# Last down-projection in Else branches, and the final normalisation in two steps, in a fused recurrent-attention and mixture-of-experts kernel

## The chip, the cores and the metric

One core of one Trainium2 chip runs the kernel. The metric is device time in microseconds, the median over runs of the same program. Engines: TensorE (PE; its weight loads are shown as PEld), VectorE (DVE), ScalarE (ACT), GpSimd (POOL) and SyncE (SP).

## What is computed

A block of 2 x 1024 tokens of width 256 is normalised by row. The normalised rows go two ways, and both results are added to the input.

```python
x = L0_attn_hidden_states
xn = _layernorm(x, axis=-1)
x = x + _L0_attn_ref(xn, ...) + _L0_ffn_ref(xn, ...)
# attention part, a recurrence along time in logarithms:
log_h = a_star + jax.lax.cumlogsumexp(log_values - a_star, axis=1)
log_h = (log_h - log_h.mean()) / jnp.std(log_h, ddof=1)
x = jnp.exp(log_h)[:, 1:, :] + hidden_states
return (x - mu) * jax.lax.rsqrt(var + LN_EPS) * ln_w + ln_b
# mixture of experts, top 2 of 8, FFN width 704:
h = jax.nn.silu(x @ w1[e].T) * (x @ w3[e].T)
out = out + h @ w2[e].T * expert_weight
```

## The kernel before

The rows of the 2048 tokens, each picked by two experts, are sorted by expert into tiles of 128 rows. How many tiles there are depends on the data: at least SURE = 33, at most NTILES = 39; here 36 are used, tiles 0 to 35. DVE works this number out on the chip and writes it to `tiles`.

For each tile j, POOL gathers its rows from `xn_dram` into `work` (`gather`, line 390, four tiles ahead); PE transposes them (`x_tile`); ACT and DVE split them into a high and a low part (`x_hi`, `x_lo`, line 967); PE does the up-projection (`up`, line 1301); ACT applies SiLU (line 608) and DVE multiplies (`gate`, line 976); PE transposes the product (`h_tile`, line 1331); ACT and DVE split it again (`h_hi`, line 603, and `h_lo`, line 971); PE does the down-projection one tile later (`down(j - 1)` in tile j, line 1319); ACT copies it with the row weights (`y_copy`, line 634), and POOL scatters it to the result with an adding indirect DMA (`scatter`, line 406). Each scatter waits for the landing of the one before, through the semaphore `s_st`.

Each engine has its own instruction queue, written out by hand in program order. Tiles 1 to 32 are unrolled. In between, the attention part runs on the same queues: `between(j)` and `after(j)` put its steps before or behind h_lo(j) on DVE. Its last step, `last_norm(m)` for m = 0 to 7, normalises two groups of 128 rows each with four operations (two of line 1069, two of line 1074) and counts up `s_p2`. When a quarter of the result is finished, POOL adds it to `out` with a plain adding DMA (`add_attention`, line 414), which waits for the last scatter, and the next scatter waits for the addition. Before the change this is done at tiles 28 (two quarters), 30 and 32 (one each). Where POOL works on an addition, the low parts of the next expert's weights (`split_due`, line 425, one piece at a time) go ahead of the scatter.

Tiles 33 to 38 are nested tests (`tail`, line 300): each engine compares the number of used tiles with j and does tile j if it is larger. The last tile's down-projection, copy and scatter come behind the whole nest, with the number of used tiles in a register: `last_down` (12 filling matmuls of line 1181, then `down`), `last_copy` (lines 736 and 739) and `end` (lines 464 to 472, the scatter at line 470).

## Time and profile before

| what | us |
|---|---|
| median of 3 runs | 352.63 (350.98 to 352.78) |
| the profiled execution's own time | 352.66 |
| its span in the profile | 350.8 |
| PE busy | 323.4 (92%) |
| DVE busy | 243.4 (69%) |
| ACT busy | 229.2 (65%) |
| POOL busy | 204.4 (58%) |

The span runs from the first to the last instruction of the program; the execution's time has some 1.8 us more around it. Busy shares are averages over stages, and what a stage waits for is read from the timeline and the chain of waits.

### The profile page before, as it was taken

The page shows a single profiled execution, that of the slowest core. Times are in us where ns is not written, and L with a number is a line of the kernel's source. Part 1 is how long each engine was busy: PE and PEld are TensorE (multiplying, and loading weights), DVE is VectorE, ACT ScalarE, POOL GpSimd, SP SyncE. Part 2 cuts the span into 40 slices and gives each one's busy share as a digit, 9 for nine tenths or more (in the row PEclk, how much of TensorE's full clock was granted, in tenths as well). Part 3 has the DMA queues.
Part 4 walks back from the last instruction along what each step waited for, and adds up shares of the span by engine and source line. Part 5 has one row for each costly group of instructions (what it writes and reads, how often), then busy time and mean ns, then how long its engine had stood idle before and what let it go on. Part 6 is the DMA issues. An engine that isn't in the chain of part 4 may idle for free.

```text
span 350.8 us, 6683 instructions
## 1 busy us (share of the span) xinstructions
PE 323.4 (92%) x1964; PEld 272.7 (78%) x1964; DVE 243.4 (69%) x430; ACT 229.2 (65%) x365; POOL 204.4 (58%) x137
## 2 busy tenths in 40 slices
PE   8998999898999999899989899999999999999950
PEld 8773474587878889788878788789998997999940
DVE  5488778989996779959889942455498767553410
ACT  2548898564889993899974349963955565443420
POOL 4600004249977763897789927765398458863531
PEclk9999969999999999999999999999999999999995
DMA  7952922005434642345346432544265265456431
GB/s 258 347 215 94 308 87 60 17 0 160 101 98 92 167 97 48 76 101 141 58 87 164 98 56 41 142 105 101 33 157 139 61 77 92 50 90 84 56 49 15
DMA packets 19087, 37.01 MB, mean 105 GB/s; under 512 B 2272, under 2 KB 13536, under 8 KB 19008
## 3 DMA queue, kind: packets, MB, share of 16 engines
q0 software_dynamic: 9168, 11.97, 21.7%
q1 hardware_dynamic: 8496, 22.56, 20.7%
q10 hardware_dynamic: 1376, 1.85, 1.5%
q8 instruction: 29, 0.48, 0.6%
q14 instruction: 18, 0.15, 0.1%
HBM read 27.45 MB, written 11.03 MB: 110 GB/s over the span
## 4 chain that ended last, share of the span: by engine, by line
PE 28%; issue 17%; ACT 15%; DVE 15%; DMA 13%; POOL 6%; POOLq 2%; ACTq 2%; DVEq 0%
PE PS L1301 9%; DMA out<-work,sidx 7%; PE PS L1195 7%; DMA out<-xrow 5%; PE PS L1319 4%; ACT L718 3%; POOL work L390 2%; PE PS L1331 2%; POOL out L406 2%; DVE tmp L976 2%; ACT tmp L608 2%; ACT L710 2%; ACT wbuf L617 2%; DVE hT L971 2%; DVE A L1013 1%
## 5 line engine op out<-in xcount | busy, mean ns | idle before, releaser
L1301 PE MATMUL PS<-wbuf,xT 128*128 128x512 f32 (+1 forms) x648 | 148.0, 382 | 4.4 <-issue 3.5
L1301 PEld LDWEIGHTS PS<-wbuf,xT 128*128 128x128 f32 x648 | 117.2, 188 | 28.3 <-issue 8.7
L425 POOL TENSOR_TENSOR wbuf<-raw,wbuf x28 | 78.7, 2822 | 27.4 <-ACT wbuf L617 26.6
L406 POOL DMA_INDIRECT out<-work,sidx x35 | 62.2, 1778 | 46.9 <-ACT work L634 24.8
L1319 PE MATMUL PS<-wbuf,hT 128*128 128x256 f32 x648 | 86.8, 288 | 0.0
L1319 PEld LDWEIGHTS PS<-wbuf,hT 128*128 128x128 f32 x648 | 79.3, 189 | 1.9 <-issue 1.9
L390 POOL DMA_INDIRECT work<-xn_dram,gidx x39 | 51.2, 1312 | 50.2 <-DVE gidx L907 36.8
L971 DVE TENSOR_TENSOR hT<-PS,hT 128x768 fp32r<-128x768 f32 x36 | 34.2, 950 | 46.1 <-ACT hT L603 45.1
L608 ACT ACTIVATE tmp<-PS 128x512 f32<-128x512 f32 x72 | 31.6, 459 | 38.8 <-PE PS L1301 38.7
L976 DVE TENSOR_TENSOR tmp<-tmp,PS 128x512 f32<-128x512 f32 x72 | 34.9, 515 | 28.8 <-ACT tmp L608 27.9
L1331 PE MATMUL PS<-ident,tmp 128*128 128x128 f32 x216 | 30.2, 276 | 6.1 <-DVE tmp L976 6.0
L634 ACT ACTIVATE work<-PS,wrow 128x256 f32<-128x256 f32 x35 | 16.4, 469 | 29.3 <-PE PS L1319 29.3
L603 ACT ACTIVATE hT<-PS 128x768 fp32r<-128x768 f32 x35 | 28.3, 810 | 10.5 <-PE PS L1331 10.5
L617 ACT ACTIVATE wbuf<-raw x28 | 30.4, 1110 | 4.7 <-issue 4.6
L1195 PE MATMUL PS<-xnT_M,small_sb 128*128 128x512 f32 x64 | 31.0, 624 | 1.7 <-ACT tmp L528 1.0
L1331 PEld LDWEIGHTS PS<-ident,tmp 128*128 128x128 f32 x216 | 23.9, 141 | 8.7 <-DVE tmp L976 7.7
L1195 PEld LDWEIGHTS PS<-xnT_M,small_sb 128*128 128x128 f32 x64 | 12.1, 202 | 14.0 <-issue 12.8
L710 ACT ACT_TABLE_LOAD x14 | 18.0, 1283 | 0.3
L718 ACT ACT_TABLE_LOAD x14 | 18.0, 1283 | 0.2
L967 DVE TENSOR_TENSOR xT<-PS,xT 128x256 fp32r<-128x256 f32 x37 | 15.5, 418 | 0.1
L575 ACT ACTIVATE xT<-PS 128x256 fp32r<-128x256 f32 x37 | 14.0, 382 | 1.6 <-PE PS L1270 1.6
L581 ACT ACTIVATE wrow<-work,first_pick 128x1 f32<-128x1 f32 x37 | 14.1, 385 | 0.0
(186 smaller groups left out, 367.3 us busy)
## 6 DMA issues: line engine op xcount, KB each, us to landing
raw<-w_main SPq DMA_DIRECT2D x24, 544.0 KB, 4.0
raw<-w_main SPq DMA_DIRECT2D x8, 416.0 KB, 3.5
xn_dram<-xrow SPq DMA_DIRECT2D x4, 516.0 KB, 5.9
out<-xrow POOLq DMA_DIRECT2D x4, 512.0 KB, 6.5
xrow<-x ACTq DMA_DIRECT2D x4, 256.0 KB, 5.8
xrow<-x SPq DMA_DIRECT2D x4, 256.0 KB, 5.2
small_sb<-small ACTq DMA_DIRECT2D x1, 768.0 KB, 8.3
work<-xn_dram,gidx POOLq DMA_INDIRECT x39, 4.1
```

The costliest lines, as they stand in the source:

```text
L390: pool.indirect_dma_start(xg[:, k, :], None, xn_dram, bass.IndirectOffsetOnAxis(gidx[:, j:j + 1], 0)).then_inc(s_gt[k], 16)
L406: pool.indirect_dma_start(out, bass.IndirectOffsetOnAxis(sidx[:, j:j + 1], 0), ysb[:, j % DEEP, :], None, compute_op=ALU.add).then_inc(s_s ...
L425: pool.tensor_tensor(lo, raw[:, ds(part, WP)], hi.bitcast(fp32), ALU.subtract).then_inc(s_w, 1)
L608: act.activation(sls[n], w1_ps[n], ACT.Silu).then_inc(s_silu, 1)
L617: act.activation(wslot(p // PIECES + 1, 0, part), raw[:, ds(part, WP)], ACT.Copy).then_inc(s_hi, 1)
L718: act.preload_act_table_set("silu_and_others")
L971: dve.tensor_tensor(hT[:, 1, :], hT_ps, hT[:, 0, :].bitcast(fp32), ALU.subtract).then_inc(s_hlo, 1)
L976: dve.tensor_tensor(g_hs[n], sls[n], w3_ps[n], ALU.mult).then_inc(s_g, 1)
L1195: ins = pe.matmul(PS[:, base + qo * CH:base + (qo + 1) * CH], wzh_sb[:, q, mat, qo * P:(qo + 1) * P], xnT[:, q, c * CH:(c + 1) * CH], star ...
L1301: ins = pe.matmul(PS[:, at:at + cols], xT[:, slot, xpart, q * P:(q + 1) * P], wbuf[:, w, wpart, q * 2 * F + at:q * 2 * F + at + cols], sta ...
L1319: ins = pe.matmul(y_ps, hT[:, hpart, c * P:(c + 1) * P], wbuf[:, w, wpart, W13 + c * D:W13 + (c + 1) * D], start=(c == 0 and hpart == 0 an ...
L1331: ins = pe.transpose(hT_ps[:, c * P:(c + 1) * P], g_h[:, a:a + P], ident[:, :])
```

## The change

Each end test gets an Else branch. If tile j isn't needed, the down-projection, copy and scatter of tile j - 1 stand in that branch with constant numbers; the same three stand behind tile 38 for the case that all tiles are used. The 12 filling matmuls, the copies of the row weights and of the scatter column, and the waits on register values go. On DVE, last_norm(6) moves from behind h_lo(30) to before it, and last_norm(7) from behind h_lo(31) to behind h_lo(30). On POOL, the third and the fourth quarter of the attention result are added together at tile 31, not at tiles 30 and 32.

```diff
-        def tail(eng, tile, end=None, drain=None):
+        def tail(eng, tile, end=None):
...
                     if j + 1 < NTILES:
                         nest(j + 1)
-                    if drain:
-                        drain(j)
+                    elif end:
+                        end(NTILES)
                     eng.nop(nofuse=True)
+                if end:
+                    with eng.Else():
+                        end(j)
+                        eng.nop(nofuse=True)
             nest(SURE)
-            if end:
-                end(used)
+            return used
...
-                    if j in (28, 30, 32):
-                        added = j // 2 - 12
+                    if j in (28, 31):
+                        added += 2
                         add_attention(j - 1, before, added)
                     done = tile(i, u, done, added, added > before)
...
             def end(used):
+
                 for k in range(DEEP):
-                    pool.wait_ge(s_gt[k], 16 * len(range(k, SURE + DEEP, DEEP)))
-                pool.tensor_copy(scol[:, 0:1], sidx[:, ds(used - 1, 1)]).then_inc(s_sc, 1)
...
-                hold(pool, s_st, whole * 16)
-                hold(pool, s_y, used + 1)
-                pool.indirect_dma_start(out, bass.IndirectOffsetOnAxis(scol[:, 0:1], 0),
-                                        hst[:, 0:D], None, compute_op=ALU.add).then_inc(s_st, 16)
-                hold(pool, s_st, 16 * used)
-            tail(pool, tile, end, drain)
+                    pool.wait_ge(s_gt[k], 16 * len(range(k, min(used + DEEP, NTILES), DEEP)))
+                scatter(used - 1, PARTS_OF_H)
+            used = tail(pool, tile, end)
+            hold(pool, s_st, 16 * used)
...
-            def last_copy(used):
-                hold(act, s_ws, used)
-                act.activation(wrow[:, NCOL:NCOL + 1], wrow[:, ds(used - 1, 1)], ACT.Copy).then_inc(s_wl, 1)
-                act.wait_ge(s_wl, 1)
-                hold(act, s_dn, used)
-                act.activation(hst[:, 0:D], y_ps, ACT.Copy, scale=wrow[:, NCOL:NCOL + 1]).then_inc(s_y, 1)
-            tail(act, tile, last_copy)
+            tail(act, tile, lambda used: y_copy(used - 1))
...
                 if 20 <= j <= 27:
                     row_stats(j - 20)
+                if j == 30:
+                    last_norm(6)
...
-                if 24 <= j <= 31:
+                if 24 <= j <= 29:
                     last_norm(j - 24)
+                if j == 30:
+                    last_norm(7)
...
-            def last_down(used):
-                warm(LAST_FILL)
-                down(used - 1, pe.snap(r_before, min_val=0, max_val=E - 1))
-            tail(pe, tile, last_down)
+            tail(pe, tile, lambda used: down(used - 1, pe.snap(r_before, min_val=0, max_val=E - 1)))
```

DVE's queue around tile 30, before: from gate(30) to h_lo(31). The names are those of the tiles in memory; hT<-PS,hT is h_lo, xT<-PS,xT is x_lo, and xrow holds the rows that last_norm works on.

```order
L976 TENSOR_TENSOR tmp<-tmp,PS 128x512 [waits silu_ready]
L976 TENSOR_TENSOR tmp<-tmp,PS 128x192 [waits silu_ready]
L967 TENSOR_TENSOR xT<-PS,xT 128x256 [waits x_hi_ready]
L971 TENSOR_TENSOR hT<-PS,hT 128x768 [waits h_hi_ready]
L1069 SCALAR_TENSOR_TENSOR xrow<-xrow,mv,small_sb 128x256 x2
L1074 SCALAR_TENSOR_TENSOR xrow<-xrow,rstd,small_sb 128x256 [waits last_norm_steps]
L1074 SCALAR_TENSOR_TENSOR xrow<-xrow,rstd,small_sb 128x256
L976 TENSOR_TENSOR tmp<-tmp,PS 128x512 [waits silu_ready]
L976 TENSOR_TENSOR tmp<-tmp,PS 128x192 [waits silu_ready]
L967 TENSOR_TENSOR xT<-PS,xT 128x256 [waits x_hi_ready]
L971 TENSOR_TENSOR hT<-PS,hT 128x768 [waits h_hi_ready]
```

The same place of DVE's queue now, from gate(30) to gate(31); lines are those of the changed kernel.

```order
L957 TENSOR_TENSOR tmp<-tmp,PS 128x512 [waits silu_ready]
L957 TENSOR_TENSOR tmp<-tmp,PS 128x192 [waits silu_ready]
L948 TENSOR_TENSOR xT<-PS,xT 128x256 [waits x_hi_ready]
L1050 SCALAR_TENSOR_TENSOR xrow<-xrow,mv,small_sb 128x256 x2
L1055 SCALAR_TENSOR_TENSOR xrow<-xrow,rstd,small_sb 128x256 [waits last_norm_steps]
L1055 SCALAR_TENSOR_TENSOR xrow<-xrow,rstd,small_sb 128x256
L952 TENSOR_TENSOR hT<-PS,hT 128x768 [waits h_hi_ready]
L1050 SCALAR_TENSOR_TENSOR xrow<-xrow,mv,small_sb 128x256 x2
L1055 SCALAR_TENSOR_TENSOR xrow<-xrow,rstd,small_sb 128x256 [waits last_norm_steps]
L1055 SCALAR_TENSOR_TENSOR xrow<-xrow,rstd,small_sb 128x256
L957 TENSOR_TENSOR tmp<-tmp,PS 128x512 [waits silu_ready]
L957 TENSOR_TENSOR tmp<-tmp,PS 128x192 [waits silu_ready]
```

Eight operations of the normalisation, four before h_lo(30) and four behind it, now stand between x_lo(31) and gate(31), and none behind h_lo(31).

POOL's queue behind the last end test, before: the end of the nest, then the last scatter (line 470).

```order
L300 UNCONDITIONAL_BRANCH x4
L300 UNCONDITIONAL_BRANCH [waits gathered2]
L300 UNCONDITIONAL_BRANCH [waits gathered1]
L464 ISA [waits gathered2,gathered3,gathered1,gathered0]
L464 COPY scol<-sidx 128x1
L467 TENSOR_LOAD tiles_whole [waits attention_added,scatter_column_ready]
L467 ISA x2
L292 REGISTER_ALU
L292 REGISTER_ALU [waits rows_added]
L470 DMA out<-hst,scol 2176x256 [waits y_copied]
```

POOL's queue now, two of the seven places where the last scatter stands (those of the last two Else branches), and the final wait.

```order
L404 DMA out<-work,sidx 2176x256 [waits rows_added,gathered3,attention_added,gathered2,y_copied,gathered1,gathered0]
L303 UNCONDITIONAL_BRANCH
L295 UNCONDITIONAL_BRANCH
L404 DMA out<-work,sidx 2176x256 [waits rows_added,gathered3,attention_added,gathered2,y_copied,gathered1,gathered0]
L303 UNCONDITIONAL_BRANCH
L287 REGISTER_ALU
L58 UNCONDITIONAL_BRANCH [waits rows_added]
```

The copy of the column, the load of a number of tiles and the register steps between the waits are gone; one DMA with constant waits is left in each branch. On PE each Else branch holds both variants of a down-projection, 18 matmuls each, so six more blocks of 36 matmuls now stand behind the tile bodies.

## Rows read from the trace of the kernel before

**Rows 1.** The page's slices: TensorE busy and its clock, tenths in 40 slices

```profile
PE   8998999898999999899989899999999999999950
PEclk9999969999999999999999999999999999999995
```

**Rows 2.** Timeline of the end: start us, us, engine, line, operation, tiles, [idle before]

```profile
327.42 0.47 ACT L634 ACTIVATE work<-PS,wrow 128x256 f32<-128x256 f32 x1 [1.48 <-PE PS L1319]
...
334.07 0.82 PE L1331 MATMUL PS<-ident,tmp 128*128 128x128 f32 x6
334.27 0.47 ACT L634 ACTIVATE work<-PS,wrow 128x256 f32<-128x256 f32 x1 [1.48 <-PE PS L1319]
...
335.77 0.96 DVE L971 TENSOR_TENSOR hT<-PS,hT 128x768 fp32r<-128x768 f32 x1 [2.79 <-ACT hT L603]
...
337.50 0.84 PE L1181 MATMUL PS<-ones_b 128*128 128x128 bf16 x12 [2.62 <-issue]
337.84 1.56 POOL L406 DMA_INDIRECT out<-work,sidx  x1 [2.51 <-DMA out<-work,sidx]
...
338.19 2.38 PE L1319 MATMUL PS<-wbuf,hT 128*128 128x256 f32 x18
...
340.66 0.47 ACT L739 ACTIVATE hst<-PS,wrow 128x256 f32<-128x256 f32 x1 [3.69 <-PE PS L1319]
342.63 1.57 POOL L470 DMA_INDIRECT out<-hst,scol  x1 [3.02 <-DMA out<-work,sidx]
```

**Rows 3.** Chain of waits at the end: start us, us, what

```profile
337.84 3.90 DMA out<-work,sidx
...
341.91 0.50 issue
342.41 0.04 POOLq L292
342.44 0.19 issue
```

**Rows 4.** Timeline of POOL, tiles 28 to 33

```profile
283.79 2.73 POOL L414 DMA_DIRECT2D out<-xrow  x2 [2.77 <-DMA out<-work,sidx]
...
294.54 1.66 POOL L406 DMA_INDIRECT out<-work,sidx  x1 [0.51 <-issue]
...
310.32 1.80 POOL L406 DMA_INDIRECT out<-work,sidx  x1 [1.73 <-issue]
...
318.96 1.38 POOL L414 DMA_DIRECT2D out<-xrow  x1 [2.86 <-DMA out<-work,sidx]
...
325.58 1.64 POOL L406 DMA_INDIRECT out<-work,sidx  x1 [3.87 <-issue]
...
329.66 1.58 POOL L406 DMA_INDIRECT out<-work,sidx  x1 [1.12 <-DMA out<-work,sidx]
```

**Rows 5.** Line 300 (end tests) and line 1284 behind it, PE's sequencer: ns min/median/max

```profile
L300 PEldq COMPARE_BRANCH  x4: 65/68/4413, 313.0 to 333.0; - x4
...
L1284 PEldq COMPARE_BRANCH  x2: 75/134/194, 338.1 to 338.4; - x2
```

**Rows 6.** Chain of waits at tile 29: scatter(28)

```profile
298.64 3.76 DMA out<-work,sidx
```

**Rows 7.** Timeline of DVE and POOL, tiles 28 to 30

```profile
288.52 3.16 DVE L1074 SCALAR_TENSOR_TENSOR xrow<-xrow,rstd,small_sb 128x256 f32<-128x256 f32 x2
288.82 5.22 POOL L425 TENSOR_TENSOR wbuf<-raw,wbuf  x2 [0.92 <-ACT wbuf L617]
...
294.96 0.87 DVE L1069 SCALAR_TENSOR_TENSOR xrow<-xrow,mv,small_sb 128x256 f32<-128x256 f32 x2
295.87 0.88 DVE L1074 SCALAR_TENSOR_TENSOR xrow<-xrow,rstd,small_sb 128x256 f32<-128x256 f32 x2
...
298.27 0.42 DVE L967 TENSOR_TENSOR xT<-PS,xT 128x256 fp32r<-128x256 f32 x1
...
299.81 3.00 POOL L425 TENSOR_TENSOR wbuf<-raw,wbuf  x1
...
301.48 0.96 DVE L971 TENSOR_TENSOR hT<-PS,hT 128x768 fp32r<-128x768 f32 x1 [2.79 <-ACT hT L603]
```

**Rows 8.** Chain of waits at tile 27: copy to scatter, landing to addition

```profile
278.15 0.48 ACT work L634
...
278.67 0.53 issue
...
283.21 0.58 issue
```

**Rows 9.** Busy time by stretch, PE; before the DMA share stands the granted clock

```profile
334.90:337.50 2.60, 0.00 (x0) 0.00 (x0) 0.96 (x1) 1.01 (x2) 0.43 (x1) 1.00 0.49 65
...
340.60:342.60 2.00, 0.00 (x0) 0.00 (x0) 0.00 (x0) 0.47 (x1) 0.00 (x0) 1.00 0.26 39
342.70:350.80 8.10, 0.00 (x0) 0.00 (x0) 0.00 (x0) 0.00 (x0) 1.51 (x1) 0.50 0.14 16
49.40:52.50 3.10, 3.09 (x4) 1.50 (x5) 0.50 0.00 0
57.00:60.00 3.00, 2.95 (x7) 1.33 (x7) 1.00 0.34 88
```

More of the change, by code:

```diff
@@ L48 @@
 FILL = 8
-LAST_FILL = 12
 BIG = 3.0e38
@@ L123, in build_program @@
         first_pick = sb("first_pick", [P, NCOL])
-        wrow = sb("wrow", [P, NCOL + 1])
+        wrow = sb("wrow", [P, NCOL])
         slot_i = sb("slot_i", [P, 3, 2 * NT], i32)
-        scol = sb("scol", [P, 1], u32)
         gidx = sb("gidx", [P, NCOL], u32)
@@ L130, in build_program @@
         tiles = sb("tiles", [P, 1], i32)
-        tiles_whole = sb("tiles_whole", [P, 1], i32)
         plan = sb("plan", [P, NCOL + 1], i32)
@@ L216, in build_program @@
         s_ws = sem("row_weights_ready")
-        s_wl = sem("last_row_weights_ready")
         s_fill = sem("x_copied_to_result")
@@ L248, in build_program @@
         s_gt = [sem(f"gathered{k}") for k in range(DEEP)]
-        s_sc = sem("scatter_column_ready")
         s_xt = sem("x_tile_transposed")
@@ L451, in _ @@
                     before = added
-                    if j in (28, 30, 32):
-                        added = j // 2 - 12
+                    if j in (28, 31):
+                        added += 2
                         add_attention(j - 1, before, added)
                     done = tile(i, u, done, added, added > before)
-            def drain(j):
-                if j + DEEP < NTILES:
-                    pool.wait_ge(s_gt[j % DEEP], 16 * ((j + DEEP) // DEEP + 1))
             def end(used):
                 for k in range(DEEP):
-                    pool.wait_ge(s_gt[k], 16 * len(range(k, SURE + DEEP, DEEP)))
-                pool.tensor_copy(scol[:, 0:1], sidx[:, ds(used - 1, 1)]).then_inc(s_sc, 1)
-                pool.wait_ge(s_sc, 1)
-                pool.wait_ge(s_ab, 16 * PARTS_OF_H)
-                whole = pool.value_load(tiles_whole[0:1, 0:1], min_val=SURE - 1, max_val=NTILES - 1)
-                hold(pool, s_st, whole * 16)
-                hold(pool, s_y, used + 1)
-                pool.indirect_dma_start(out, bass.IndirectOffsetOnAxis(scol[:, 0:1], 0),
-                                        hst[:, 0:D], None, compute_op=ALU.add).then_inc(s_st, 16)
-                hold(pool, s_st, 16 * used)
-            tail(pool, tile, end, drain)
+                    pool.wait_ge(s_gt[k], 16 * len(range(k, min(used + DEEP, NTILES), DEEP)))
+                scatter(used - 1, PARTS_OF_H)
+            used = tail(pool, tile, end)
+            hold(pool, s_st, 16 * used)
         @block.scalar
@@ L867, in tile_experts @@
                 step(dve.tensor_scalar(tiles[:, :], tend[:, E - 1:E], float(SURE), None, ALU.max))
-                step(dve.tensor_scalar(tiles_whole[:, :], tiles[:, :], -1, None, ALU.add))
                 dve.sem_inc(s_eid, 1)
```

## The prediction

> **What bounds the kernel now.** The page's slices come first [rows 1]: TensorE's clock stands at full nearly throughout, and only the last two slices are thin. So the body of the run belongs to TensorE, and what this change touches is the last 25 us and the two ends that meet there. The timeline of the end comes next [rows 2]. Call a tile's down-projection down(j); 36 tiles are used, 0 to 35. TensorE transposes tile 35 at 334.07 to 334.89, then does nothing until the 12 filling matmuls at 337.50, runs down(35) at 338.19 to 340.57, ScalarE copies it at 340.66 to 341.13, and GpSimd starts its scatter at 342.63. The copy was therefore ready 1.50 us before that scatter. The chain of waits says why [rows 3]: scatter(34) starts at 337.84, takes 3.90 to land, at 341.74, and only then do GpSimd's register waits and their 0.50 and 0.19 us of issue run. At the very end two queues race: scatters, one at a time, on GpSimd; and TensorE's end test with down(35) behind it. The scatters win by little. After 342.63 come 8.2 us (the landing, about 3.8, and the shutdown) that the change leaves alone.
>
> Where the scatters fell behind is seen on GpSimd's timeline [rows 4]. The last addition of the attention result is issued at 318.96 and scatter(31) follows at 325.58, 6.62 later. From there on one scatter follows the other at 329.66 - 325.58 = 4.08 us, less than the 6.85 us between the copies of two tiles (327.42 and 334.27 [rows 2]), so the backlog shrinks but is not gone by tile 35.
>
> TensorE's end test is one branch of 4413 ns begun at 333.0 [rows 5], so it ends at 337.45, where tests that fall through take 65 to 68 ns. It starts while the transposes are still queued; 2.6 us of it show as TensorE idle.
>
> **The change, part by part.** *Two additions instead of three.* Nothing moves before tile 30: the first pair is still issued at tile 28. GpSimd's schedule from there, worked out: scatter(28) starts at 298.64 and lands 3.76 later, at 302.40 [rows 6]; the weight piece it overlaps ends at 299.81 + 3.00 = 302.81 [rows 7]. At tile 30 no addition is due, so the gather (about 0.3 of gap, 1.0 of work, 0.3 of gap, as between the gathers and scatters of this engine) is followed by scatter(29) at about 304.5 instead of 310.32. It lands at 308.3, and the addition follows 0.6 later (283.17 to 283.79 in [rows 8]), at 308.9. Both parts go out together. The pair of tile 28 was issued at 283.79 and its scatter followed at 294.54 [rows 4], 10.75 later; I take that for this pair too. Its bounds are 6.62, if the second addition hides behind the first, and 2 x 6.62 = 13.2, if they share nothing. Scatter(30) is then at 308.9 + 10.75 = 319.7, and scatter(34), four steps on, at 319.7 + 4 x 4.08 = 336.0 instead of 337.84, landing at 339.9. With the bounds it lands between 339.4 (scatter(34) can't start before its copy, ready at 334.74, and 0.8 of issue) and 342.3.
>
> *Normalisation before h_lo(30).* VectorE idles 2.79 us ahead of h_lo(30), from 298.69 on [rows 7]. The four operations of last_norm(6) take 0.87 + 0.88 [rows 7] and would fit. But the last of them would start at about 299.9 (298.6 + 0.87 and half of 0.88), and GpSimd's weight piece starts at 299.81. What happens then stands in the same trace: at tile 28 the same pair of operations took 3.16 us instead of 0.88, with the piece starting at 288.82 in the middle of it [rows 7]. I take the blocked case: the operation ends with the piece, near 303.1, h_lo(30) starts 1.5 late, last_norm(7) runs to 305.7, and gate(31) starts at 305.6, over a microsecond late. Behind that gate wait the transposes of tile 31 (they start behind down(30), at about 306.6, so they are covered) and x_lo(32), now done at 306.9. In the trace of before x_lo(31) was done at 298.69 and VectorE was then free, so this wait of up(32) is a new one, close to its start after down(30) and the transposes: I put +0.2 on TensorE for it, an estimate. Bounds: 0, if the operation slips ahead of the piece, and 2.6, the length of a piece (two of them take 5.22 [rows 7]), if the next one, due about 305.7, also catches last_norm(7).
>
> *Else branches on GpSimd and ScalarE.* The copy of the row weights and the copy of the scatter column and the waits on registers go. Both lie between the last down-projection's start and the landing at 341.74, beside other waits, and are worth nothing. The waits on registers stood between landing and scatter: 341.74 to 342.63. With constants, a copy is followed by its scatter after 0.80 (278.63 to 279.43 [rows 8]), since the separate wait still has 0.53 of issue behind it. So with the copy at 341.13 the scatter would be at 341.93. That is later than the 339.9 + 0.3 at which the scatters would be ready: **the path moves over to TensorE**. This much is -0.70.
>
> *Else branches on TensorE.* The last test is still false at the same instruction of the same queue. It still has to go past three tile bodies, now past three Else bodies too (the order shows them). I take its 4413 ns as they are. Bounds: 0.1, as the other tests, and twice, 8.8. Whoever waits for it: down(35), nothing else. The 12 fills go; down(35)'s own branch only starts at 338.1 [rows 5], and its first matmul at 338.19, so the fills delayed nothing: 0, bound 0.69.
>
> *What the fills covered.* Without them TensorE stands idle from 334.89 to about 338.15, 3.3 us instead of 2.6. The clock's rows [rows 9]: granted 1.00 (2.4 GHz) through the 2.60 idle before the fills; and after down(35) idle from 340.6 at 1.00 for 2.00 us and at 0.50 (1.2 GHz) directly after. So an idle stretch of just over 2 us has cost the level once and one of 2.6, ended by fills, has not. 3.3 us ended by work that itself is only 2.4 us long is on the bad side of both. What the lower level costs: 4 matmuls of line 1195 begun in 3.10 us at 0.50 against 7 in 3.00 at 1.00 [rows 9], near a factor of two; so down(35) grows by at most 2.38 x 1 = 2.4 and by 0 at least. I take 1.1: the level falls, but with part of down(35) done. The fall may come before or after the start of down(35), so that the middle is the fairest choice.
> The Trainium skill ("TensorE: Matmul & The Clock Gate", "Why this matters for your kernels") tells one to leave TensorE no long idle gap between bursts of matmuls, since the gate then goes back to half rate. By that rule the whole of down(35) could be at half rate, which would be 354.5; by the 2.60 us row alone nothing would happen, which would be 352.2.
>
> **Sum.** -0.70 (register waits) + 0.2 (tile 31) + 1.1 (clock) = +0.6 on a profiled execution of 352.66 (its span of 350.8 and some 1.8 around it), which is the median, 352.63, to within 0.03. **Forecast 353.2 us**: no difference that can be told.
>
> **Rivals.**
> 1. *The clock holds.* For it: the 2.60 us row. Against it: the fall soon after 340.57. Then -0.5: 352.2. Chance 0.25; the forecast itself, with the clock falling in part or whole, has 0.45.
> 2. *A second hold at tile 30 or 31, slower.* The weight piece after scatter(29) starts before the last operation of last_norm(7), due at 305.2, and holds it until the piece ends. For it: VectorE's operations of this kind were held as often as they started within a piece. Against it: about 0.5 us of distance, and that is the point from which it decides. TensorE then loses 2.6 instead of 0.2: 352.66 - 0.70 + 2.6 + 0.5 (clock, half of 1.1) = 355.1. Chance 0.12.
> 3. *The pair of additions is slow.* At its bound of 13.2, scatter(34) lands at 342.3, the last scatter is at 342.6, and all gains are gone; TensorE's losses are covered: 352.7. It decides from a pair of 12.5 on. Chance 0.11; no change.
> 4. *The test becomes cheap, faster.* If the Else branch is reached without the 4.4 us, down(35) starts when its input is ready, 335.8, and the scatters bound, at about 340.2: 352.66 - 2.4 = 350.3. For it: the ScalarE and GpSimd tests of the same program are short. Against it: TensorE's jump is longer than before. Chance 0.07.
> The Trainium skill ("Runtime: NRT & Kernel Launch", "Instruction fetch mechanics") says that a taken branch whose target is not in the fetched pages waits for a fetch. By it the 4413 ns stay, since the target lies farther off than before.
>
> **How the numbers follow.** A measurement of this kernel tells about 0.5%, 1.8 us, from no change. The forecast, rival 1 and rival 3 are within it; rival 2 is above, rival 4 below; a full-rate loss of the whole of down(35), 354.5, is just above too and holds some of the forecast's chance. Faster 0.07, same 0.78, slower 0.15. The range runs from 351.3 (rival 1 with the lower of the runs shown) to 355.1 (rival 2) and leaves out rival 4 and the double jump.
>
> **What the changed kernel would show.** Scatter(30) near 319.7 and scatter(34) near 336.0, both additions issued near 308.9; last_norm(6) lasting past 302.8 and up(32) 0.2 late; on TensorE a last test of some 4.4 us, an idle time of 3.3 us before down(35), and down(35) in more than 2.4 us with a granted clock under 1.00; the last scatter 0.8 after the copy. The forecast is wrong if TensorE's test is much shorter or longer, if TensorE idles over 1 us at tiles 30 to 32, or if the last scatter still waits for a landing.

## The result, and the profile after

| | median, us | ratio to before, 95% interval |
|---|---|---|
| changed kernel, 6 runs | 360.2 (357.19 to 362.81) | 1.0205 [1.017, 1.0239] |
| before, beside it, 6 runs | 352.26 (350.98 to 352.89) | |
| profiled execution of after | 358.37, its span 356.6 | |

The change costs 7.9 us, 2%. The forecast was 353.2 us with no difference that can be told, so it was wrong, and the time lies 5 us above its range. The ratios leave out runs over 1.5% above the fastest of the same kernel: one run of the changed kernel here (362.81), and seven of the ten of `pad` below.

The page's slices of the changed kernel, to be held against [rows 1]:

```profile
PE   7898999798999999998998999899999999699940
...
PEclk9999989999999999999999999999999999899965
```

There are now two thin places: slice 35 of 40 (303 to 312 us), where nothing was thin before, with the clock at 0.8, and the end, where the clock is down one slice earlier. The first place, on the timeline of the changed kernel (L1050 and L1055 are last_norm, L423 a weight piece, L412 the additions, L957 the gate, L952 h_lo, L1316 the transposes of the product, L1286 up):

```profile
298.62 3.48 DVE L1055 SCALAR_TENSOR_TENSOR xrow<-xrow,rstd,small_sb 128x256 f32<-128x256 f32 x2
...
298.80 3.01 POOL L423 TENSOR_TENSOR wbuf<-raw,wbuf  x1
...
302.01 0.94 DVE L952 TENSOR_TENSOR hT<-PS,hT 128x768 fp32r<-128x768 f32 x1
...
303.78 4.30 DVE L1055 SCALAR_TENSOR_TENSOR xrow<-xrow,rstd,small_sb 128x256 f32<-128x256 f32 x2
...
304.32 3.07 POOL L423 TENSOR_TENSOR wbuf<-raw,wbuf  x1
...
308.00 0.94 DVE L957 TENSOR_TENSOR tmp<-tmp,PS 128x512 f32<-128x512 f32 x2
308.38 2.72 POOL L412 DMA_DIRECT2D out<-xrow  x2 [0.98 <-DVE xrow L1055]
...
308.73 1.54 PE L1316 MATMUL PS<-ident,tmp 128*128 128x128 f32 x6 [2.84 <-DVE tmp L957]
...
309.93 4.80 PE L1286 MATMUL PS<-wbuf,xT 128*128 128x512 f32 x18
```

Both pairs of L1055 that should take 0.88 [rows 7] lasted until just behind a weight piece: 3.48 and 4.30 us. The first delays only h_lo(30). The second delays gate(31), and TensorE stands idle for 2.84 us waiting for it. After that its own work is slow too: the six transposes take 1.54 instead of 0.82 [rows 2], the 18 matmuls of up(32) 4.80 where those of up(35) take 4.09.

The end of the changed kernel, the same places as in [rows 2] (L1304 is down, L622 the copy, L404 the scatter), and its last end tests, to be held against [rows 5]:

```profile
337.48 0.82 PE L1316 MATMUL PS<-ident,tmp 128*128 128x128 f32 x6
...
338.96 1.56 POOL L404 DMA_INDIRECT out<-work,sidx  x1 [5.28 <-ACT work L622]
...
340.60 0.19 PEld L1304 LDWEIGHTS PS<-wbuf,hT 128*128 128x128 f32 x1 [2.54 <-issue]
343.04 4.00 PE L1304 MATMUL PS<-wbuf,hT 128*128 128x256 f32 x18 [4.74 <-issue]
...
347.08 0.47 ACT L622 ACTIVATE work<-PS,wrow 128x256 f32<-128x256 f32 x1 [7.93 <-PE PS L1304]
348.36 1.55 POOL L404 DMA_INDIRECT out<-work,sidx  x1 [7.84 <-ACT work L622]
```

```profile
L295 PEldq COMPARE_BRANCH  x7: 65/175/3434, 316.5 to 344.1; - x7
```

The last scatter waits for the copy alone; scatter(34) was issued 9.4 us before it. TensorE's test took 3434 ns, not 4413, and was over at 340.00. But then the engine issued one weight load at 340.60 and nothing more until 343.04: a second stall, inside the Else branch. Last, down(35) took 4.00 us instead of 2.38. TensorE by stretch, as in [rows 9] (granted clock before DMA share):

```profile
305.70:308.50 2.80, 0.20 (x2) 0.00 (x0) 2.80 (x3) 0.47 (x1) 1.81 (x2) 0.93 0.28 40
308.60:312.60 4.00, 3.87 (x15) 3.35 (x16) 1.64 (x4) 0.81 (x1) 3.60 (x3) 0.64 0.66 83
...
338.40:340.40 2.00, 0.00 (x0) 0.00 (x0) 0.96 (x1) 0.75 (x1) 1.44 (x1) 1.00 0.00 0
340.40:343.00 2.60, 0.00 (x0) 0.19 (x1) 0.00 (x0) 0.00 (x0) 0.11 (x1) 0.85 0.50 63
343.00:347.10 4.10, 4.00 (x18) 3.71 (x17) 0.00 (x0) 0.02 (x1) 0.00 (x0) 0.50 0.01 4
```

Granted 0.50 is 1.2 GHz, 1.00 is 2.4 GHz. A stretch with a value between holds both. So the clock falls late in the idle stretch ahead of 308.7 and stays low for a part of what follows; it is full for the first 2 us behind the last transposes, falls before TensorE resumes at 343.0, and all of down(35) runs at 0.50.

To add the losses up I cut the end into three pieces. The body is from the start of up(30) to the end of the transposes of tile 35; it holds the same 264 matmuls in both kernels (busy time of PE by stretch: first before, then after).

```profile
293.30:334.90 41.60, 41.41 (x264) 37.74 (x264) 18.97 (x36) 18.73 (x38) 25.92 (x18) 1.00 0.46 65
```

```profile
292.57:338.30 45.73, 42.89 (x264) 38.84 (x264) 24.83 (x36) 18.59 (x38) 25.97 (x18) 0.96 0.45 62
```

| piece | before | after | difference | forecast |
|---|---|---|---|---|
| body | 41.41 | 45.73 | +4.3 | +0.2 |
| to the end of the last copy | 6.24 (334.89 to 341.13) | 9.25 (338.30 to 347.55) | +3.0 | +1.1 |
| to the start of the last scatter | 1.50 | 0.81 | -0.7 | -0.7 |
| sum | 49.15 | 55.79 | +6.6 | +0.6 |

The span grew by 5.8 only, because up(30) starts 0.9 earlier in this execution, at 292.57 instead of 293.48; in a second profiled execution of the same kernel it is at 291.86.

### The profile page after: what moved, and what is told of

It is laid out like the page before. It is cut to its first block, busy times and chain, and to the rows that moved or that the text cites. A ratio compares the mean times of both kernels' runs of the same rounds, so it can differ in the third digit from the quotient of the medians.

```text
span 356.6 us, 6652 instructions
## 1 busy us (share of the span) xinstructions
PE 324.5 (91%) x1952; PEld 273.3 (77%) x1952; DVE 247.5 (69%) x429; ACT 229.0 (64%) x364; POOL 206.6 (58%) x136
## 4 chain that ended last, share of the span: by engine, by line
PE 48%; DVE 22%; ACT 12%; issue 9%; DMA 3%; POOL 2%; ACTq 1%; POOLq 0%; DVEq 0%; SPq 0%
PE PS L1286 20%; PE PS L1304 11%; PE PS L1180 7%; PE PS L1316 4%; DVE xrow L1055 4%; DVE tmp L957 3%; DVE hT L952 2%; ACT L706 2%; ACT hT L591 2%; DVE xnT_M L964 1%; DVE A L994 1%; ACT tmp L596 1%; POOL wbuf L423 1%; DMA xrow<-x 1%; PE PS L1210 1%
## 5 line engine op out<-in xcount | busy, mean ns | idle before, releaser
L1286 PE MATMUL PS<-wbuf,xT 128*128 128x512 f32 (+1 forms) x648 | 148.7, 383 | 4.3 <-issue 3.3
L1286 PEld LDWEIGHTS PS<-wbuf,xT 128*128 128x128 f32 x648 | 117.8, 189 | 28.3 <-issue 8.3
L404 POOL DMA_INDIRECT out<-work,sidx x36 | 65.4, 1816 | 59.3 <-ACT work L622 37.8
L423 POOL TENSOR_TENSOR wbuf<-raw,wbuf x28 | 82.1, 2940 | 24.4 <-ACT wbuf L605 23.0
L1304 PE MATMUL PS<-wbuf,hT 128*128 128x256 f32 x648 | 88.4, 291 | 4.7 <-issue 4.7
L1304 PEld LDWEIGHTS PS<-wbuf,hT 128*128 128x128 f32 x648 | 81.0, 192 | 6.7 <-issue 6.7
L388 POOL DMA_INDIRECT work<-xn_dram,gidx x39 | 49.6, 1273 | 49.1 <-DVE gidx L888 35.9
L952 DVE TENSOR_TENSOR hT<-PS,hT 128x768 fp32r<-128x768 f32 x36 | 34.2, 950 | 41.9 <-ACT hT L591 41.0
L957 DVE TENSOR_TENSOR tmp<-tmp,PS 128x512 f32<-128x512 f32 x72 | 35.0, 516 | 32.4 <-ACT tmp L596 31.5
L622 ACT ACTIVATE work<-PS,wrow 128x256 f32<-128x256 f32 x36 | 16.9, 470 | 37.3 <-PE PS L1304 37.3
L1316 PE MATMUL PS<-ident,tmp 128*128 128x128 f32 x216 | 30.9, 280 | 8.6 <-DVE tmp L957 8.5
L1316 PEld LDWEIGHTS PS<-ident,tmp 128*128 128x128 f32 x216 | 24.3, 143 | 11.4 <-DVE tmp L957 10.5
L1055 DVE SCALAR_TENSOR_TENSOR xrow<-xrow,rstd,small_sb 128x256 f32<-128x256 f32 x16 | 17.9, 1158 | 0.3
```

What stands on the lines that cost most here:

```text
L388: pool.indirect_dma_start(xg[:, k, :], None, xn_dram, bass.IndirectOffsetOnAxis(gidx[:, j:j + 1], 0)).then_inc(s_gt[k], 16)
L404: pool.indirect_dma_start(out, bass.IndirectOffsetOnAxis(sidx[:, j:j + 1], 0), ysb[:, j % DEEP, :], None, compute_op=ALU.add).then_inc(s_s ...
L423: pool.tensor_tensor(lo, raw[:, ds(part, WP)], hi.bitcast(fp32), ALU.subtract).then_inc(s_w, 1)
L952: dve.tensor_tensor(hT[:, 1, :], hT_ps, hT[:, 0, :].bitcast(fp32), ALU.subtract).then_inc(s_hlo, 1)
L957: dve.tensor_tensor(g_hs[n], sls[n], w3_ps[n], ALU.mult).then_inc(s_g, 1)
L1055: ins = dve.scalar_tensor_tensor(xn[:, t, :], xn[:, t, :], rstd[:, t:t + 1], lnwb[:, 1, :], ALU.mult, ALU.add)
```

## The experiments

My theory after the result: two causes that have nothing to do with each other. **A**, last_norm held by GpSimd's weight pieces (held: the operation ends only when the piece has ended), idles TensorE at tile 31 and costs it the clock. **B**, the Else branches lie where the fetch of TensorE's instructions stalls twice, and without the fills down(35) meets the low clock. The rivals: one cause alone; or the two additions together, or the missing fills alone, cost the time. "up(30) to h35" below is the body of the table above, "h35 to copy" its second piece; h35 stands for the end of the transposes of tile 35. Runs of before beside these had medians of 350.85 (19 runs), 351.3 (21) and 351.75 (29), and spread from 349.75 to 353.28.

**One half each.** `only_norm` is the kernel before with the normalisation and the additions of after; `only_else` is after with these as they were before.

```diff
-                    if j in (28, 30, 32):
-                        added = j // 2 - 12
+                    if j in (28, 31):
+                        added += 2
...
+                if j == 30:
+                    last_norm(6)
```

> The kernel before with one part of the change: last_norm(6) before h_lo(30), last_norm(7) behind it, additions at tiles 28 and 31; the end stays as it was. Theory: the weight pieces on GpSimd hold VectorE twice (3.5 us and 4.3 us for two operations that take 0.88 alone), TensorE idles 2.8 us before the transposes of tile 31 and then runs for some 3.4 us at the lower clock; together 4.3 us, of which the end had 0.8 us of slack: about 3.6 us slower than the kernel before, near 356. Rival: all of the loss is at the end tests, and this kernel is within 1 us of the kernel before.

> The kernel before with the other part of the change: Else branches, constant waits, no filling matmuls; normalisation and additions as before. Theory: from the transposes of tile 35 to the end of down(35) it takes 8.7 us instead of 5.7 (a second stall of the instruction stream of 2.5 us, and the lower clock for 1.6 us), minus 0.7 us of register waits: about 2.4 us slower, near 355. Rival: the end costs nothing that the first part did not cause, and this kernel is the same as the one before or 0.7 us faster.

Measured: only_norm 355.16 (351.43 to 355.98, 10 runs), ratio 1.0077 [1.0035, 1.0119]; only_else 355.41 (354.59 to 356.07, 4 runs), 1.0117 [1.0072, 1.0163], which is more than the 2.4 us expected of it. The timeline of only_norm has both holds and the wait (L1074 last_norm, L1335 the transposes), that of only_else has neither, but the late down(35) (L1300):

```profile
299.18 3.90 DVE L1074 SCALAR_TENSOR_TENSOR xrow<-xrow,rstd,small_sb 128x256 f32<-128x256 f32 x2
...
304.77 4.28 DVE L1074 SCALAR_TENSOR_TENSOR xrow<-xrow,rstd,small_sb 128x256 f32<-128x256 f32 x2
305.31 3.05 POOL L425 TENSOR_TENSOR wbuf<-raw,wbuf  x1
...
309.35 2.72 POOL L414 DMA_DIRECT2D out<-xrow  x2 [0.98 <-DVE xrow L1074]
...
309.70 1.46 PE L1335 MATMUL PS<-ident,tmp 128*128 128x128 f32 x6 [3.24 <-DVE tmp L976]
```

```profile
339.69 3.46 PE L1300 MATMUL PS<-wbuf,hT 128*128 128x256 f32 x18 [6.00 <-issue]
```

Each half loses on its own, 4.3 and 4.6 us by the medians, 2.7 and 4.1 by the ratios, where the whole loses 7.9 and 7.2: two causes, which rules out the rivals with one. In only_norm the body takes 46.45 us (+5.0); in only_else h35 to copy takes 9.97 (+3.7). only_norm's ten runs fall in two clusters, three at 351.4 to 352.4 and seven at 353.9 to 356.0. A hold that is sometimes missed would do that; no profile caught such an execution, so it isn't shown. The clock is a rival for a part of it: the 19 runs of before beside it fall in two clusters too, ten at 349.8 to 350.9 with a mean granted clock of 0.981 to 0.986 and nine at 352.0 to 352.9 with 0.971 to 0.977.

only_norm still has the old end with its waits on registers, and its copy ends at 344.84 with the scatter at 345.62, 0.78 later. With constants it is 0.81. Behind a landing there is no difference either: 0.89 from landing to last scatter in before, and 0.97 with constants in best3 and move7 below. So the waits on registers cost nothing that constants give back; they showed before only because a landing came last [rows 3].

**Where the Else code lies.** `pad` is after with 16 matmuls that never run, in the branch for tile 38: they shift the Else branches by 32 instructions. `fill` is after with the 12 fills back, ahead of each Else's down.

```diff
                     elif end:
+                        if eng is nc.tensor:
+                            unused_fill(eng)    # 16 matmuls, tile 38 isn't used
                         end(NTILES)
```

```diff
+            def last_down(used):
+                warm(LAST_FILL)
+                down(used - 1, pe.snap(r_before, min_val=0, max_val=E - 1))
```

> The changed kernel with 16 filling matmuls (32 instructions) in the branch for tile 38, which never runs here; they only move the Else branch of tile 36 by 32 instructions. Theory: the 2.5 us stall within down(35) comes from a boundary between two fetched blocks of instructions, which now falls elsewhere; it goes, TensorE runs the 18 matmuls without a gap behind the branch, and the kernel is 2.5 to 4 us faster than the changed one, near 357. Rival: the stall belongs to the taken branch or to the static waits; then nothing changes and it stays near 360.

> The changed kernel with the 12 filling matmuls back ahead of down(35), in each Else branch. They also move the branch by 72 instructions, out of the reach of the block boundary. Theory: no stall and full clock in down(35) (2.4 us instead of 4.0): 4 us faster than the changed kernel, near 356, and 1 to 1.6 us faster than the kernel that only moves the branch. Rival: the fills only cost their own time, and the two are the same.

Timelines of pad (L1310 is down) and of fill (L1167 the fills, L1305 down):

```profile
341.39 2.96 PE L1310 MATMUL PS<-wbuf,hT 128*128 128x256 f32 x18 [2.57 <-issue]
```

```profile
338.96 0.84 PE L1167 MATMUL PS<-ones_b 128*128 128x128 bf16 x12 [1.61 <-issue]
...
339.61 2.36 PE L1305 MATMUL PS<-wbuf,hT 128*128 128x256 f32 x18
```

In pad the test takes 3.73 and down(35) follows 0.69 behind it: the second stall is gone though the same instructions run, and h35 to copy is 6.04 us instead of 9.25. Without fills and without the stall the clock still falls within down(35), which takes 2.96. In fill h35 to copy is 5.14, and down(35) is back at 2.36 at the full clock: here the fills arrive after 1.61 us of idle. Both keep their holds (3.42 and 4.30 in pad, 3.41 and 4.30 in fill). fill's median is 355.45 (353.24 to 356.27, 5 runs), 1.011 [1.0066, 1.0154]: half of the loss is left, that of A. pad's is 354.73 (10 runs: 349.03, 350.84, and eight from 354.25 to 356.18). Its ratio, 1.0004 [0.9947, 1.006], rests on the three lowest of them, so I read pad by its trace alone. That fill is 1 to 1.6 us faster than pad, as expected, is seen in the traces only (0.9 us less from h35 to copy); the medians don't show it.

**The same stall put into the kernel before.** If a place in the code makes the second stall, the old end must get it when it is shifted there. `before_cross` is the kernel before with 111 unused matmuls, 222 instructions, in the branch for tile 38.

> The kernel before, with 111 filling matmuls (222 instructions) in the branch for tile 38, which never runs here; they only move the code behind the nest so that the block boundary falls between the 12 fills and down(35). Theory: a stall of some 2.5 us appears between fills and down(35), in a kernel that has none of the change; 0.8 us of it is covered: 1.7 us slower than the kernel before, up to 3.3 with the lower clock. Rival: where the code stands does not matter, and it is the same as the kernel before.

The chain of waits of before_cross at the end (L1187 the fills, L1325 down(35)):

```profile
334.58 2.42 issue
337.00 0.84 PE PS L1187 x12
337.84 2.89 issue
340.73 4.10 PE PS L1325 x18
```

354.97 us (354.61 to 356.1, 4 runs), 1.0111 [1.0081, 1.0141]: 3.7 us slower than before, a little over the 3.3 that were expected at most. Nothing that runs is different from before; 2.89 us of stall appear between the fills and down(35), and down(35) then runs at the low clock. h35 to copy is 10.80 us. So the position alone does it. Counted in TensorE's instruction stream, the end code of the kernel before, of pad and of fill begins at places 124, 145 and 185 of a block of 256, and none has the stall; in after it begins at 113 and stalls within some 8 instructions, and in before_cross at about 90 and stalls behind the 24 of the fills. A boundary near 120 fits all five. Counted from the start of the program instead, the two stalls lie at the same place, since before_cross has 222 more instructions than before ahead of its end code and after some 245; so one boundary there is shown, and not that it comes back every 256. The Trainium skill ("Runtime: NRT & Kernel Launch", "Instruction fetch mechanics") says that instructions come in blocks of 256 and that a jump out of the fetched ones waits for a fetch. The wait of 3.3 to 4.4 us at the jump agrees; the block's length isn't tested here. It also says that the cost of crossing a boundary is mostly hidden, and right behind such a jump it isn't: 2.4 to 3.0 us in five profiles (after, after_again, only_else, after_psum, before_cross). That the stall is a fetch is the reading of the Trainium skill; the runs show only that it goes by the place of the code.

**Away with the hold.** `after_psum` is after with the weights of last_norm(6) and (7) read from PSUM instead of SBUF; ScalarE copies them there at tile 27. Order and instructions on DVE stay. (`before_psum` is the kernel before with this for last_norm(4) to (7).)

```diff
+                ln = ln_ps if m in (6, 7) else [lnwb[:, 0, :], lnwb[:, 1, :]]
...
-                    ins = dve.scalar_tensor_tensor(xn[:, t, :], xn[:, t, :], rstd[:, t:t + 1], lnwb[:, 1, :],
+                    ins = dve.scalar_tensor_tensor(xn[:, t, :], xn[:, t, :], rstd[:, t:t + 1], ln[1],
```

> The changed kernel, with the scale and shift of last_norm(6) and last_norm(7) read from PSUM, where ScalarE copies them at tile 27, so that these operations of VectorE have one input in SBUF and not two. Theory: what holds VectorE during a weight piece of GpSimd is the second SBUF input; the pairs take about 0.9 us again instead of 3.4 and 4.3, TensorE has no idle time before the transposes of tile 31, and the kernel is about 4 us faster than the changed one, near 355 to 356, with the end still slow. Rival: any VectorE operation on SBUF is held, or the operations are just late; then nothing changes.

> The kernel before, with the scale and shift of last_norm(4) to (7) read from PSUM. Theory: the pair at tile 28 takes 0.9 us instead of 3.16 and TensorE gains 1.2 us there, but the path runs over the additions and scatters, which nothing here moves: the same time as before, within 0.5 us. Rival: TensorE sets the end, and it is 1.2 us faster.

Timeline of after_psum (L1065 the second pair of last_norm, L425 the piece, L1326 the transposes, L1296 up, L1314 down):

```profile
297.53 0.88 DVE L1065 SCALAR_TENSOR_TENSOR xrow<-xrow,rstd,PS 128x256 f32<-128x256 f32 x2
297.59 3.01 POOL L425 TENSOR_TENSOR wbuf<-raw,wbuf  x1
...
304.66 0.82 PE L1326 MATMUL PS<-ident,tmp 128*128 128x128 f32 x6
...
305.23 4.09 PE L1296 MATMUL PS<-wbuf,xT 128*128 128x512 f32 x18
...
339.72 4.00 PE L1314 MATMUL PS<-wbuf,hT 128*128 128x256 f32 x18 [5.65 <-issue]
```

The pair of last_norm(6) runs through the piece in 0.88 us; that of last_norm(7), no longer late, is over at 302.15, before the next piece at 303.12. TensorE has no wait at tile 31 and no slow matmul; the body is 42.56 us instead of 45.73. That is still 1.15 above before: TensorE stands idle for 0.91 us ahead of up(33), and in best below for 0.65, for a reason that the traces don't show. The end stalls as in after (h35 to copy 10.17). 355.25 (353.29 to 356.47, 4 runs), 1.0118 [1.0077, 1.0159]: the other half of the loss is left, that of B. The two repairs are thus complements. What held the pair was its second input in SBUF: in the same place of the queue, beside the same piece, it isn't held with one.

The Trainium skill ("SBUF — State Buffer", "SBUF: two separate sides") has the rule: a VectorE instruction with two SBUF inputs and a GpSimd one that reads SBUF exclude each other for a whole instruction, and whichever starts first goes. The exclusion agrees. "First" doesn't fit the recorded starts: the operation begun at 303.78 in after was held until 307.68, though the piece's record starts only at 304.32; GpSimd's recorded spans are rough.

before_psum lost instead of gaining: 352.47 (351.28 to 354.61, 8 runs), 1.0042 [1.0016, 1.0068]. Its TensorE is 1.2 us ahead at the last transposes, but its last scatters wait for landings, one of them following the last by 5.3 instead of the usual 4.1, which is about what was lost. Its down(35) met the low clock (3.57), but its copy was ready 3.5 us before the last scatter. So TensorE's gain has no way to the end here; why that one landing was late stays open.

**Both repairs.** `best` is fill with the PSUM weights for last_norm(4) to (7). `else_fill` is only_else with the fills. `move7` is fill with last_norm(7) in another place: both last_norm(6) and (7) directly before an h_lo.

```diff
-                if j == 30:
-                    last_norm(6)
+                if j in (30, 31):
+                    last_norm(j - 24)
```

> The changed kernel with the fills back in the Else branches (which also moves them away from the block boundary) and with the scale and shift of last_norm(4) to (7) read from PSUM. Theory: no hold, no second stall, full clock: scatter(34) about 1.8 us earlier than in the kernel before, the copy of tile 35 about 1.2 us earlier, the last scatter 0.8 behind the copy; 1.9 us faster than the kernel before (0.5%). Rival: the taken branch of the end test grows with what it jumps over, and it is the same or slower.

> Only the Else branches and constant waits, with the fills kept in each branch (the block boundary lies elsewhere); normalisation and additions as in the kernel before. Theory: only the 0.5 to 0.7 us between the last landing and the last scatter are gained: 0 to 0.7 us faster than the kernel before, too little to be told. Rival: the end tests themselves cost something, and it is over 1 us slower.

> The changed kernel with the fills back in the Else branches, and last_norm(7) moved on, from behind h_lo(30) to before h_lo(31), behind gate(31) and x_lo(32); last_norm(6) stays before h_lo(30), all inputs in SBUF. Theory: the hold costs TensorE only because gate(31) waits behind it; last_norm(7) is still held by the second weight piece, but with gate(31) already done, and TensorE's idle time of 2.8 us before the transposes of tile 31 goes: 4 us faster than the kernel with fills alone, near 351. Rival: the four operations held twice are late wherever they stand, and the addition at tile 31 or h_lo(31) is late for it: no gain.

| kernel | median, us | ratio to before |
|---|---|---|
| best, 12 runs | 350.59 (348.58 to 352.16) | 0.9981 [0.9956, 1.0006] |
| move7, 10 runs | 351.48 (350.28 to 353.05) | 0.9981 [0.996, 1.0003] |
| else_fill, 12 runs | 352.31 (350.48 to 352.86) | 0.9996 [0.9972, 1.002] |

Timeline of the end of best (L1315 down, L407 scatters), and of move7 around its last_norm(7) (L1051 and L1056):

```profile
335.20 2.36 PE L1315 MATMUL PS<-wbuf,hT 128*128 128x256 f32 x18
337.61 0.47 ACT L625 ACTIVATE work<-PS,wrow 128x256 f32<-128x256 f32 x1 [3.93 <-PE PS L1315]
338.89 1.55 POOL L407 DMA_INDIRECT out<-work,sidx  x1 [3.85 <-ACT work L625]
```

```profile
298.60 0.88 DVE L1056 SCALAR_TENSOR_TENSOR xrow<-xrow,rstd,small_sb 128x256 f32<-128x256 f32 x2
...
299.08 3.15 POOL L424 TENSOR_TENSOR wbuf<-raw,wbuf  x1
...
304.55 3.98 DVE L1051 SCALAR_TENSOR_TENSOR xrow<-xrow,mv,small_sb 128x256 f32<-128x256 f32 x2
304.75 3.09 POOL L424 TENSOR_TENSOR wbuf<-raw,wbuf  x1
```

All three are back at the time of before, and none beats it by more than the measurement tells; the 1.9 us expected of best didn't come. else_fill says that the Else branches, once the code doesn't stall twice, gain nothing by themselves that can be told. Its fills didn't keep the clock (L1163 the fills, L1301 down(35)):

```profile
336.42 1.10 PE L1163 MATMUL PS<-ones_b 128*128 128x128 bf16 x12 [2.16 <-issue]
...
337.27 3.71 PE L1301 MATMUL PS<-wbuf,hT 128*128 128x256 f32 x18
```

They came after 2.16 us of idle, and down(35) took 3.71. In before_psum it was 2.27 and 3.57; in before 2.62 and 2.38, in move7 2.40 and 2.37. So at 2.2 to 2.6 us of idle ahead of the fills the clock was kept in two profiles and lost in two, and the length of the idle stretch didn't decide it.

What move7 says is that a hold is harmless where VectorE has the room: L1051 is held for 3.98 us, but gate(31) is already behind it, and the body takes 41.42 us. Its rival held in part: the addition waits for the held pair and goes out at 309.75 (306.94 in best), and the last scatter, at 341.73, waits for a landing again, 1.8 us behind its copy. Its first pair began in the same place as in the others and was not held, with the piece starting 0.08 behind its second operation; in after_again (below) and only_norm the piece started 0.09 behind it, and it was held. So whether the hold strikes turns on a difference too small to be read from these records. best's profiled execution is 3.9 us under that of before and its median 0.7; the profiled one was among its fastest, and up(30) starts 3.0 us earlier in it, of which the hold at tile 28 explains 1.2.

**The additions one by one.** `best3` is best with the third and fourth quarter added at tiles 30 and 31 instead of together.

```diff
-                    if j in (28, 31):
-                        added += 2
+                    if j in (28, 30, 31):
+                        added += 2 if j == 28 else 1
```

> The kernel of the last run of the set before (Else branches with fills, scale and shift in PSUM, normalisation as in the changed kernel), but the third and fourth quarter are added at tiles 30 and 31, one each. Theory: the addition at tile 30 goes out about 4 us earlier than the pair of tile 31 and the scatters need no pair to wait for, but the path runs over TensorE's end test and the copy by now: the same as with the pair, within 0.5 us. Rival: the scatters still bound, and one at a time moves the end by more than 1 us either way.

353.44 (351.12 to 355.8, 12 runs), 1.0044 [1.0017, 1.007]: by the ratios slower than best by 0.6%, 2.2 us, where I had expected it no slower. The timeline of best3's scatters (L415 an addition, L407 scatters):

```profile
314.58 1.39 POOL L415 DMA_DIRECT2D out<-xrow  x1 [3.48 <-issue]
...
321.21 1.63 POOL L407 DMA_INDIRECT out<-work,sidx  x1 [3.85 <-issue]
...
343.67 1.56 POOL L407 DMA_INDIRECT out<-work,sidx  x1 [3.24 <-DMA out<-work,sidx]
```

The second single addition again costs 6.6 us of GpSimd's queue, scatter(30) is at 321.21 (in best 316.41) and the last scatter waits for a landing again; one of the steps before it took 5.4 us instead of 4.1, as in before_psum. So adding two quarters together doesn't cost time, which was the last of the rivals: the pair at tile 31 is the one part of the change that works as forecast.

**The changed kernel once more**, for its median against its profile.

> The changed kernel once more, unaltered, for more runs of it beside runs of the kernel before. The losses that were found (two held pairs of last_norm, 4 to 5 us of TensorE; a second stall of 2.5 to 2.9 us in the Else branch and a down-projection at the lower clock) sum to about 5.8 us on the span, so this theory expects a median near 351.3 + 5.8 = 357.1 us, between 356 and 359, and in the profiled execution both stalls and both held pairs again. Rival: the first set's median of 360.2 is what this program takes and there is a further loss of some 3 us that its profiled execution (358.4) did not show; then the median is again at or above 359.5, and the profile shows a loss in a place other than the three.

359.52 (358.3 to 359.86, 5 runs), 1.0221 [1.0194, 1.0247]; its profiled run has a span of 357.7. The median is the rival's, but the places are mine. Timeline, and TensorE by stretch:

```profile
308.45 1.54 PE L1316 MATMUL PS<-ident,tmp 128*128 128x128 f32 x6 [3.26 <-DVE tmp L957]
...
309.64 6.29 PE L1286 MATMUL PS<-wbuf,xT 128*128 128x512 f32 x18
```

```profile
309.60:313.60 4.00, 4.00 (x11) 3.16 (x10) 0.96 (x1) 0.81 (x1) 2.31 (x2) 0.50 1.04 138
```

The wait at tile 31 was 3.26, and up(32) took 6.29 where it took 4.80 in the first profile and 4.09 at full clock: the low clock lasted longer. The body is 47.66, +6.2, of which 3.26 wait, 0.72 transposes and 2.20 up(32). With h35 to copy of 9.20 (+3.0) and -0.7 the three pieces sum to +8.5, against 359.52 - 351.31 = 8.2 of median. I had left out that what an idle stretch costs afterwards varies from run to run, here 1.4 or 2.9 us.

## Why the prediction was wrong

Two terms of its sum failed: the +0.2 for the normalisation, where the runs showed +4.3 to +6.2, and the end of TensorE, where a test of unchanged length and +1.1 for the clock stood against a second stall of 2.4 us that the sum didn't have.

- **Two additions instead of three: right in kind.** Additions at 308.38 (forecast 308.9), scatter(30) at 319.55 (319.7), 11.17 later (10.75). That the first two times fit so closely is in part luck: this execution is 0.9 us early, and what released the additions was the held pair of last_norm(7), not the landing of scatter(29). scatter(34), forecast at 336.0, was at 338.96, bound no longer by landings but by its copy, which TensorE's loss made late. Rival 3 fell.
- **Else branches on GpSimd and ScalarE: the -0.70 is right, its name is not.** Copy to scatter is 0.81 as forecast, but with register waits it is 0.78: the gain was the landing that no longer came last, so it belongs to the additions.
- **Normalisation before h_lo(30): the step that failed most.** I had the first hold right (h_lo(30) at 302.01, the pair until 302.09) and put +0.2 on what followed; it was 4.3. The second hold was rival 2, with a chance of 0.12. Its argument was a distance of about 0.5 us between the last operation and the next piece. But I had only placed scatter(29) by estimate (304.5; 303.27 measured, with all times of this execution 0.9 lower) and the piece follows it by 1.05; half a microsecond of distance out of two estimated queues was no reason for 0.12. Once late by the first hold, the second pair stood in the path of the next piece in every profiled execution of this order (after twice, only_norm, pad, fill). Its price was too small as well: rival 2 took 2.6 and nothing for the clock at that place, while 2.84 us of idle and 1.43 of slow matmuls were the first execution's bill, 3.26 and 2.92 the second's. The clock argument that I used at the end, rows of 2 to 3 us of idle, applied here just as well.
- **Else branches on TensorE: the second failed step.** The taken branch I took at 4.41; it was 3.43. I had bounded the jump and not asked what the code behind it does. The second stall put first matmul 3.04 us behind the end of the test where before it was 0.74 with fills between.
- **What the fills covered: right in kind.** The low clock came and cost 1.6 instead of 1.1, on the whole of down(35), as the second stall made the idle stretch 4.74 us instead of 3.3. pad, without that stall, shows the term alone: 2.57 us of idle and +0.6. My bound of 2.4 for the whole at half clock was too high too. Rival 1, the clock that holds, fell. Together the end is -0.86 (test) + 2.30 (second stall, less the fills) + 1.62 (clock) = +3.06, where +3.01 was measured. The fills, which I valued at nothing, do two jobs: they can keep the clock (not in else_fill and before_psum), and here their mere length moved the code off the boundary.
- **The test becomes cheap** (rival 4) didn't happen; it took 3.3 to 4.4 us in every profile of the study. What sets it within these bounds isn't shown.

Not settled: why the recorded start of a held operation can lie 0.54 us before that of the piece which holds it (that distance was the same in after, only_norm and fill), whether only_norm's two clusters are holds hit and missed, what decides whether the low clock costs 1.4 or 2.9 us behind nearly the same idle stretch, and whether fills keep the clock. Not tried: the whole of after with the pieces of GpSimd moved instead of the normalisation.

## What to carry to other kernels

Before an operation with two SBUF inputs is moved on VectorE, look at what GpSimd works on at that time, and price the case that it is held for GpSimd's whole operation, with every later one behind it; an input in PSUM takes the hold away. An idle stretch of TensorE can cost more than its own length: behind 2.8 to 3.3 us of it the slow matmuls cost 1.4 to 2.9 us more here. Filling matmuls may prevent that, and didn't always. Behind a jump far forward the position of the code counts: look for a gap right behind the first instructions there, and shift the code by unused instructions to see whether the gap moves.

## What the runs showed of the hardware

- A held VectorE operation ended 0.29 us after the piece's recorded end in all nine holds at tiles 30 and 31 of after, after_again, only_norm, fill and move7 (for instance 307.39 and 307.68 in after); pairs with one PSUM input took 0.86 to 0.88 beside the same pieces.
- 32 instructions that never run moved 3.2 us of TensorE's time (9.25 to 6.04 from h35 to copy), 222 of them 4.6 us the other way (6.24 to 10.80).
- The same 18 matmuls of up(32) took 4.09, 4.80, 5.19 and 6.29 us behind idle stretches of 0, 2.84, 3.24 (only_norm) and 3.26 us.
- Twelve fills behind 2.62 and 2.40 us of idle were followed by a down(35) of 2.38 and 2.37 us, behind 2.16 and 2.27 by one of 3.71 and 3.57.
